# Two-layer graph attention and a graph convolution on one core: four adjacency loads with buffers of their own, and another order at the start

## The reference, cut to what matters

```python
h = relu(layernorm(x))                       # x: 4096 x 128
for W, b in ((W0, b0), (W1, b1)):            # two attention layers
    att = h @ h.T / sqrt(128)
    A = softmax(where(adj > 0, att, -9e15), axis=1)     # adj: 4096 x 4096, mostly 0
    A = 0.5 * A + 0.5 * eye;  the first nf1 rows become rows of eye
    h = relu(A @ (h @ W.T + b))
x = x + h
h = relu(layernorm(x))
a_norm = D^-1/2 (adj + eye) D^-1/2           # D: row sums of adj + eye
out = x + (a_norm @ h) @ W.T + b
```

## Time and profile before

| | us |
|---|---|
| median of 3 runs | 1009.04 (1003.52, 1009.04, 1010.0) |
| profiled execution, its own time | 1005.73 |
| its span | 1003.9 |
| TensorE busy in it | 960.1 (96%) |
| VectorE, ScalarE, GpSimd busy | 540.2, 444.2, 82.3 |
| mean granted clock of TensorE | 0.988 |

### The profile page before, as it was taken

One profiled execution on the slowest core, in us unless ns is written; L12 is line 12 of the kernel. 1 busy time (PEld: TensorE's weight loads), 2 busy tenths in 40 slices (PEclk: granted clock), 3 DMA queues, 4 the chain that ended last, 5 costly groups with the idle time before them and its releaser, 6 DMA issues.

```text
span 1003.9 us, 16182 instructions
## 1 busy us (share of the span) xinstructions
PE 960.1 (96%) x6598; PEld 872.5 (87%) x6598; DVE 540.2 (54%) x962; ACT 444.2 (44%) x641; POOL 82.3 (8%) x75
## 2 busy tenths in 40 slices
PE   3999999999999999998999999999999998699998
PEld 2899999999999999988999999999999997577776
DVE  3555444454545453545554765755666777734443
ACT  3655666666666666621111221222121222475564
POOL 3761000000000000005000000000000000400000
PEclk9899999999999999999999999999999999889999
DMA  9976888888989988750000000000000001300000
GB/s 240 217 168 171 196 235 207 218 214 224 212 216 212 220 215 223 189 173 2 1 1 12 11 2 11 12 1 12 11 12 12 14 19 42 101 0 32 11 22 22
DMA packets 101968, 103.26 MB, mean 103 GB/s; under 512 B 72960, under 2 KB 79872, under 8 KB 101888
## 3 DMA queue, kind: packets, MB, share of 16 engines
q1 hardware_dynamic: 101376, 101.94, 40.4%
q0 software_dynamic: 80, 0.02, 0.1%
q10 hardware_dynamic: 432, 0.20, 0.1%
...
## 4 chain that ended last, share of the span: by engine, by line
PE 92%; DVE 3%; DMA 2%; ACT 1%; issue 1%; SPq 1%; DVEq 0%; ACTq 0%
PE pAcc L1120 36%; PE pMisc L1187 10%; PE pS L1039 9%; PE pS L1037 9%; PE pS L1038 9%; PE pS L1267 6%; PE pS L1268 5%; PE pTurn L1174 5%; DMA adjT<-nat 1%; PE pMisc L1253 1%; DMA x_scratch<-x_block 1%; DVE x_block L812 1%; ACT adj_wide L602 1%; DVE prob L919 0%; ACT aggT L608 0%
## 5 line engine op out<-in xcount | busy, mean ns | idle before, releaser
L1120 PE MATMUL pAcc<-feat,prob 128*128 128x129 f32 x3200 | 393.8, 276 | 9.1 <-DVE prob L898 6.9
L1120 PEld LDWEIGHTS pAcc<-feat,prob 128*128 128x128 f32 x3200 | 382.6, 192 | 22.7 <-DVE prob L898 7.3
L898 DVE TENSOR_TENSOR prob<-prob,adjT 128x1024 f32<-128x1024 f32 x128 | 156.8, 1225 | 202.8 <-ACT prob L550 195.9
L570 ACT ACTIVATE prob<-pS 128x1024 f32<-128x1024 f32 x72 | 73.7, 1024 | 308.9 <-PE pTurn L1174 273.3
L550 ACT ACTIVATE prob<-pS 128x1024 f32<-128x1024 f32 x128 | 130.9, 1022 | 140.8 <-PE pS L1039 140.8
L1037 PE MATMUL pS<-high 128*128 128x512 f32 x400 | 174.6, 436 | 0.0
L1039 PE MATMUL pS<-high,low 128*128 128x512 f32 x400 | 158.6, 396 | 0.0
L1038 PE MATMUL pS<-low,high 128*128 128x512 f32 x400 | 156.6, 391 | 0.0
L506 ACT ACTIVATE nat<-chunk 128x1024 uint8<-128x1024 f32 x128 | 134.4, 1050 | 13.8 <-DMA adjT<-nat 11.6
L1267 PE MATMUL pS<-adj_wide,z_high 128*128 128x512 f32 x256 | 106.7, 417 | 17.8 <-DVE adj_wide L1010 9.3
L1187 PE MATMUL pMisc<-feat,turned_prob 128*128 128x129 f32 x896 | 118.4, 275 | 0.0
...
## 6 DMA issues: line engine op xcount, KB each, us to landing
chunk<-in_adj_dram SPq DMA_DIRECT2D x128, 512.0 KB, 4.5
x_in<-in_x_dram SPq DMA_DIRECT2D x8, 256.0 KB, 6.2
adjT<-nat SPq DMA_TRANSPOSE x128, 3.4
x_block<-in_x_dram SPq DMA_DIRECT2D x8, 256.0 KB, 2.8
x_scratch<-x_block SPq DMA_DIRECT2D x8, 256.0 KB, 2.0
x<-x_scratch SPq DMA_DIRECT2D x8, 256.0 KB, 4.7
hiT_scratch<-highT SPq DMA_DIRECT2D x7, 256.0 KB, 5.0
loT_scratch<-lowT SPq DMA_DIRECT2D x7, 256.0 KB, 4.9
```

The source lines that it names most:

```text
L898: nc.vector.tensor_tensor(pr, pr, adj_unit(b, u), ALU.mult).then_inc(prob_ready[L], 1)
L1120: mm = nc.tensor.matmul(pAcc[:, t // 2, (t % 2) * W:(t % 2 + 1) * W], prob[:, buf, h, t * P:(t + 1) * P], feat[:, 2 * u + h, :], start=(fi ...
```

## The change

Seven edits, all of them in the start and in block 0 of layer 0:

1. The first four casts write to `nat_first`, four buffers of their own, and load 3 has a buffer of its own, `chunk_last`. Both lie in the room of `adjT`'s block 4. Load k now stands for one of four semaphores.
2. SyncE starts with x 0, adj 0, adj 1, x 1, adj 2, adj 3, x 2 and the biases. Nothing follows turn 0; x 3 follows turn 1; adj 4 and x 4 follow turn 2; adj 5, adj 6 and x 5 follow turn 3; from turn 4 on adj k + 3 follows turn k as before, and x k + 2 up to x 7.
3. ScalarE casts load 1 ahead of `high_of_x(0)`, and makes `high_of_x(1)` behind cast 3.
4. VectorE makes `low_of_x(0)` ahead of `x_normal(1)`, and takes the variances of group 2 behind `W1T_low`.
5. `EARLY` is 3: group 2 is normalised by VectorE, behind `keep_feat(0, 0)` and ahead of the first mask, and no more by GpSimd.
6. TensorE makes the scores of unit 0 ahead of `turn_h(1)`.
7. The turns of groups 2 to 7 stand behind the mix of their unit, and no more ahead of it.

```diff
--- before.py
+++ after.py
@@ -149,6 +149,10 @@
         nf_rows, _, o = place("nf_rows", [P, 1], F32, offset=o)
         node_f, _, o = place("node_f", [P, NJ], F32, offset=o)
         assert o <= adjT_at + 6 * blk
+        o = adjT_at + 4 * blk
+        nat_first, _, o = place("nat_first", [P, RT, CC], U8, offset=o)
+        chunk_last, _, o = place("chunk_last", [P, CC], F32, offset=o)
+        assert o <= adjT_at + 5 * blk
 
         def bank(name, shape):
             return ctx.enter_context(nc.psum_tensor(name, shape, F32))
@@ -175,7 +179,7 @@
         feat_made, feat_ready, feat_totalled = each("feat_made", 2), each("feat_ready", 2), each("feat_totalled", 2)
         tiny_made, tiny_ready, feat_ones = each("tiny_made", 2), each("tiny_ready", 2), sem("feat_ones")
 
-        chunk_loaded, cast_done, mask_landed = each("chunk_loaded", CHUNKS), sem("cast_done"), each("mask_landed", RT)
+        chunk_loaded, cast_done, mask_landed = each("chunk_loaded", CHUNKS + 1), sem("cast_done"), each("mask_landed", RT)
 
         scores_ready, exp_ready, prob_ready, prob_used = (each("scores_ready", 2), each("exp_ready", 2),
                                                           each("prob_ready", 2), each("prob_used", 2))
@@ -201,7 +205,7 @@
 
         GROUPS = NJ // RT
 
-        EARLY = 2
+        EARLY = 3
 
         AHEAD = 4
 
@@ -227,6 +231,13 @@
 
         def adj_tile(b, t):
             return adj_unit(b, t // 2)[:, t % 2, :]
+
+        def chunk_of(k):
+
+            return chunk_last[:, :] if k == CHUNKS else chunk[:, (k - (k > CHUNKS)) % CHUNKS, :]
+
+        def nat_of(k):
+            return nat_first[:, k, :] if k < RT else nat[:, k % NATS, :]
 
         def casts_before(g):
 
@@ -304,9 +315,10 @@
             def load_adj(k):
                 b, c, tt = load_of(k)
                 t = RT * b + tt
-                wait(sp, cast_done, k - CHUNKS + 1)
-                sp.dma_start(chunk[:, k % CHUNKS, :], adj_rows[t // 2, t % 2, :, c * CC:(c + 1) * CC])\
-                    .then_inc(chunk_loaded[k % CHUNKS], 16)
+                if k > CHUNKS:
+                    sp.wait_ge(cast_done, k - CHUNKS + (k > 2 * CHUNKS))
+                sp.dma_start(chunk_of(k), adj_rows[t // 2, t % 2, :, c * CC:(c + 1) * CC])\
+                    .then_inc(chunk_loaded[k % (CHUNKS + 1)], 16)
 
             def turn_adj(k):
                 b, c, tt = load_of(k)
@@ -314,7 +326,7 @@
                 if k == 5 * UNITS:
                     sp.wait_ge(rows_ready, 1)
                     sp.wait_ge(feat_ready[0], GROUPS)
-                sp.dma_start_transpose(adjT[:, b, RT * c:RT * (c + 1), tt * P:(tt + 1) * P], nat[:, k % NATS, :].bitcast(U16))\
+                sp.dma_start_transpose(adjT[:, b, RT * c:RT * (c + 1), tt * P:(tt + 1) * P], nat_of(k).bitcast(U16))\
                     .then_inc(mask_landed[tt], 16)
 
             def store_h1(b):
@@ -330,19 +342,20 @@
 
             load_rows(0)
             load_adj(0)
+            load_adj(1)
             load_rows(1)
-            load_adj(1)
             load_adj(2)
+            load_adj(3)
             load_rows(2)
-            load_rows(3)
             for row, b in ((bias0, b0), (bias1, b1)):
                 sp.dma_start(row[:, :], b.rearrange("(a d) -> a d", a=1).broadcast_to([P, P])).then_inc(bias_loaded, 16)
             for k in range(LOADS):
                 turn_adj(k)
-                if k + CHUNKS < LOADS:
-                    load_adj(k + CHUNKS)
-                if k + 4 < GROUPS:
-                    load_rows(k + 4)
+                for kk in {0: (), 1: (), 2: (4,), 3: (5, 6)}.get(k, (k + CHUNKS,)):
+                    if kk < LOADS:
+                        load_adj(kk)
+                if k > 0 and k + 2 < GROUPS:
+                    load_rows(k + 2)
                 at_unit = k - LEAD
                 if at_unit >= UNITS and at_unit % UNITS == 9:
                     store_h1(at_unit // UNITS - 1)
@@ -500,10 +513,10 @@
             def cast_adj(k):
                 b, c, tt = load_of(k)
                 t = RT * b + tt
-                act.wait_ge(chunk_loaded[k % CHUNKS], 16 * (k // CHUNKS + 1))
-                if k >= NATS:
+                act.wait_ge(chunk_loaded[k % (CHUNKS + 1)], 16 * (k // (CHUNKS + 1) + 1))
+                if k >= RT + NATS:
                     act.wait_ge(mask_landed[(k - NATS) % RT], 16 * ((k - NATS) // RT + 1))
-                nc.scalar.activation(nat[:, k % NATS, :], chunk[:, k % CHUNKS, :], ACT.Copy,
+                nc.scalar.activation(nat_of(k), chunk_of(k), ACT.Copy,
                                      accum_out=deg_part[:, t, c:c + 1]).then_inc(cast_done, 1)
 
             def high_of_x(grp):
@@ -515,11 +528,11 @@
             nc.scalar.activation(W0T_high[:, :], pMisc[:, 0:P], ACT.Copy).then_inc(w_high_ready, 1)
             nc.scalar.activation(W1T_high[:, :], pMisc[:, P:2 * P], ACT.Copy).then_inc(w_high_ready, 1)
             nc.scalar.activation(WgT[:, :], pMisc[:, 2 * P:3 * P], ACT.Copy).then_inc(w_high_ready, 1)
+            cast_adj(1)
             high_of_x(0)
-            cast_adj(1)
-            high_of_x(1)
             cast_adj(2)
             cast_adj(3)
+            high_of_x(1)
 
             def keep_acc(L, b):
                 act.wait_ge(prob_used[L], (b + 1) * UNITS)
@@ -693,17 +706,18 @@
             nc.vector.tensor_tensor(W0T_low[:, :], pMisc[:, 0:P], W0T_high[:, :].bitcast(F32), ALU.subtract)\
                 .then_inc(w_low_ready, 1)
             x_variances(1)
+            low_of_x(0)
             x_normal(1)
-            low_of_x(0)
-            x_variances(2)
             dve.wait_ge(w_high_ready, 3)
             nc.vector.tensor_tensor(W1T_low[:, :], pMisc[:, P:2 * P], W1T_high[:, :].bitcast(F32), ALU.subtract)\
                 .then_inc(w_low_ready, 1)
+            x_variances(2)
             low_of_x(1)
             dve.wait_ge(bias_loaded, 32)
             dve.wait_ge(feat_ones, 1)
             dve.wait_ge(consts_ready, 4)
             keep_feat(0, 0)
+            x_normal(2)
 
             def tiny(L):
                 dve.wait_ge(tiny_made[L], 1)
@@ -1085,7 +1099,6 @@
             for k in range(3):
                 nc.tensor.transpose(pMisc[:, k * P:(k + 1) * P], w_in[:, k, :], ident[:, :]).then_inc(w_turned, 1)
             turn_h(0)
-            turn_h(1)
 
             def unit_scores(b, u):
                 rows = slice(b * BW, (b + 1) * BW)
@@ -1134,8 +1147,6 @@
 
             def prepare_at(u):
 
-                if u % 2 == 0 and u // 2 + 2 < GROUPS:
-                    turn_h(u // 2 + 2)
                 if u % 2 == 1 and u // 2 + 1 < GROUPS:
                     make_feat(0, u // 2 + 1)
                 if u == 14:
@@ -1148,6 +1159,7 @@
 
             def attention(L):
                 scores(L, 0)
+                turn_h(1)
                 pe.wait_ge(w_low_ready, 2)
                 make_feat(0, 0)
                 for b in range(NB):
@@ -1160,6 +1172,8 @@
                         if b > 0 and u == 5:
                             turn_h1(b - 1)
                         mix(L, b, u, u % 2, g)
+                        if b == 0 and u % 2 == 0 and u // 2 + 2 < GROUPS:
+                            turn_h(u // 2 + 2)
 
             def turn_exp(g, k):
```

## The result

The changed kernel takes 999.75 us (median of 20 runs, 996.14 to 1007.29), the kernel before 1002.49 (median of 20, 1000.55 to 1010.04). The ratio, from comparisons side by side, is 0.9961, with a 95% interval of 0.9942 to 0.998: 3.9 us faster, between 2.0 and 5.8; the two medians differ by 2.7. I had forecast 1005.1 and a step of -2.0 us. The three runs of before that I had were high by chance (median 1009.04): its median over 20 is 6.5 us lower. The profiled execution of the changed kernel has a time of 999.73 us; it is compared with the 1005.73 of before.

What follows compares the result with a forecast made beforehand. It took the DMA queue ahead of turn 3, which holds up the first mix, as the bound. Queue -3.1, turn +0.4 and clock +0.7 gave -2.0 us, from a mean of 1007.1 to 1005.1; range 1001.5 to 1008.5, over all cases 999.5 to 1010.0.

Steps and rivals of the forecast that it cites:

- The order at the start (edits 3, 4, 6): Reordered scores, casts and VectorE work before the first mask: all ends in the wait for turn 3, so nothing.
- The queue, not the issue, bounds turn 3: SyncE's DMA queue at the start: what stands ahead of turn 3 sets its landing, not when it is issued.
- Later. Nothing: From turn 4 on SyncE, casts and buffers run as before: no change in time.
- The queue: Edits 1 and 2: 1.05 MB less ahead of turn 3, landing at 22.2 instead of 25.3 us, -3.1 us.
- Cast 3 now waits for adj 3 alone: ScalarE at the start: turn 3 can be issued at 18 us even if adj 3 lands at 16.
- The turn behind the mix, +0.4 us: Edit 7, TensorE: four matmuls of group 2's turn leave the wait and stand behind the first mix, +0.4 us.
- The cover that I gave for the other turns: Later turns: next exponential about 0.4 us late, VectorE's mask leaves 0.9 us to spare, so no cost.
- The clock, +0.7 us: TensorE at the first mix: more work at the lower clock level, +0.7 us, middle of 0 and +1.5.
- one of the signs of being wrong that I had named: A new wait of VectorE or ScalarE on the pairs of units behind the first mix.
- the hole closes: Low DMA rate from 8 to 16 us (136 GB/s) lifts: -7.2 us, 999.9 from the mean; chance 0.12.
- slower by the clock: Before unit 0's mix: clock +1.5, turn +0.4; with turn 3 as late as before +1.9 us, 1009.0; chance 0.14.
- the change doesn't reach turn 3: SyncE's slow issue of turns 1 to 3 holds turn 3 to 23.5 to 24 us: -0.4 us, 1006.7; chance 0.17.

Runs made afterwards that it cites:

- late gather: The changed kernel with GpSimd's gather of the first column of adj issued behind the rows of group 4, at 36.6 us: 999.35 us, ratio 0.9959.
- The engines' order: Edits 3 to 7 on the kernel before, without edits 1 and 2: 1004.8 us, ratio 1.0005.
- three kernels without a gain: Edits 1 and 2 on the kernel before (ratio 1.000), edit 1 on the kernel before (1.0006), the changed kernel with edit 3 undone (1.0009).

## Why the prediction was right and wrong

The step that failed is the term "The order at the start (edits 3, 4, 6)", put at nothing, and with it the premise "The queue, not the issue, bounds turn 3": with edit 3 undone the gain is gone, 1003.52 us against 1000.07. "Later. Nothing" failed too. The forecast was a step of 2.0 us where the runs have 3.9, and most of the miss in the predicted time is the level that it starts from.

**The queue: the size right, the mechanism in part.** Forecast -3.1 us for turn 3; measured -2.8 by the means. But in all 18 profiles turn 3 lands 4.2 to 5.0 us behind its issue, whether that comes at 13.44 us (late gather) or at 21.03 (before). By the means the issue moved by 3.3 us (20.05 to 16.72), and the landing followed. So "The queue, not the issue, bounds turn 3" does not hold. In the chains shown above the issue is set by cast 3, and cast 3 by the landing of turn 1 before and by that of load 3 now. Megabytes ahead act on the landing of load 3; that their sum gave the right size is partly luck. I had presumed that the issue is early enough, since "Cast 3 now waits for adj 3 alone". It holds only with edit 3. Without it cast 3 still waits for `high_of_x(1)`, and that for TensorE.

**"The order at the start (edits 3, 4, 6)" at nothing.** I costed these edits by the path from the scores to the mask, where they do have cover, and not by the path from the casts through SyncE to the turns. Edit 3 moves an instruction that waits for TensorE out of the way of two that feed the DMA queue, and with buffers and loads in the new order it decides the gain: 1003.52 us without it, 1000.07 with it, on one chip. The engines' order gave no gain without the buffers either. So buffers and edit 3 are both needed. The share of edit 2 is not shown, since no kernel had edits 1 and 3 with the old order of the queue. Nor is it shown that edits 4 to 6 add anything: edits 1 to 3 alone gave 0.9981, the change 0.9952 to 0.9961, and the intervals overlap.

**The turn behind the mix, +0.4 us:** it stands in the chain with 0.44 us, as forecast, and undoing it changed nothing in the median. The cover that I gave for the other turns has a slip: 1.83 + 0.44 less 1.0 is 1.27, not 1.4, so the exponential would come 0.2 us late and not 0.4. Nothing hangs on it.

**The clock, +0.7 us: the wrong sort of number.** At the start it is not a fixed price. The clock fell there in all three profiles of before, and in the changed kernel twice whole, once in part, once not at all, with a first mix of 3.81, 2.93 or 2.05 us. From the first mix to that of unit 3 the changed kernel takes 0.45 us more in the mean (15.26 against 14.81); the turn's 0.4 and the clock's 0.7 would make that 1.1. The Trainium skill (TensorE: Matmul & The Clock Gate, Part 1) has a monitor that runs free of the kernel. Two of the profiles of the changed kernel agree with that: the first mixes start at the same 22.85 us, the pauses ahead of them are 3.18 and 2.97 us, and only behind the shorter one did the clock fall, for a part of the mix. The two whole falls don't decide it, for they came with longer pauses, 4.90 and 5.86 us.

**"Later. Nothing": wrong twice.** First, the exponential of unit 2 behind cast 7 made TensorE wait 0.93 us in one profile, one of the signs of being wrong that I had named. I had checked ScalarE around 48 us, in the steady part, and not the exponentials of units 1 and 2, where its casts come two at a time. Second, of the 4.4 us between the means of the profiles 2.1 aren't in the start. I split each run's time into the loss to the clock, as above, and the rest. Over the 103 runs of before beside the experiments (one more took 5240.11 us and is left out): 1004.31 us in the mean, of which 10.88 are that loss. Over 32 runs of the changed kernel: 1000.11, of which 8.12. So counted, 1.4 us of 4.2 are work and waits, and 2.8 are clock. The count makes the clock too dear, because a fall costs nothing while TensorE waits: the one at the start of the first profile of before counts 3.4 us and cost 1.8. Over the 103 runs a microsecond of counted loss goes with 0.65 us of time, over the 32 with 0.57. By these slopes 1.6 to 1.8 us of the 4.2 are clock, and the other 2.4 to 2.6 are about what the start gained in the profiles. 25 of 103 runs of before lost 14 us or more to it, and 2 of 32 of the changed kernel. The profiles put a part of this at the start of the convolution. That the change causes it there has not been shown: nothing is edited there, and three kernels without a gain had the short stretch too. A kernel whose stretches lie 2 us earlier could meet the falls differently, or it is chance; I have no experiment that tells these apart, and it stays open.

**The sum.** For the start I had -2.0, and at the 2900th matmul the profiles have -2.3 in the mean, with two errors that cancel in part (the queue 0.3 less, the clock less dear): that is luck. The runs have -3.9, with an interval that begins at -2.0. The predicted 1005.1 lies 5.4 above the median: 4.6 because the four known times of before averaged 1007.1 where its median is 1002.49, and 0.7 because the medians differ by 2.7 and not 2.0.

**The rivals.** 1, the hole closes: it did not, with 162 to 169 GB/s in four profiles against 136, 209 and 151. The argument against it was the right one. The Trainium skill (DMA: Bandwidth & Descriptors, Queues, rings and completion order) has the DMA engines go round the queues that have work. That moving the gather away gave 284 GB/s agrees with it. 2, slower by the clock: turn 3 came 2.8 us earlier, beyond the point of 1.9 from which it would not decide. 3, the change doesn't reach turn 3: it does not hold for the change (issue at 16.55), but it is what happens without edit 3. I had its price, and looked for its cause in the issue of turns (6.14 us for turns 0 and 1, where with the gather moved away they took 2.89: a mark of the hole) and not in ScalarE.
